# One pipeline over all 96 tiles of a six-layer network, with the attention product written transposed and the bursts of small matmuls joined

## What is computed

```python
qkv = x @ Wqkv;  q, k, v = jnp.split(qkv, 3, -1)      # 16 heads of 64
q = l2norm(q) * qs;  k = l2norm(k) * ksc              # then rotary, with scale
# local_attention: windows of 32 queries, each with its own and the previous 32 keys
sim = jnp.einsum('bhwie,bhwje->bhwij', bq, bk2) * 8.0
sim = jnp.where(mask, -jnp.finfo(sim.dtype).max, sim)
attn = jax.nn.softmax(sim, -1)
out = jnp.einsum('bhwij,bhwje->bhwie', attn, bv2)
x = x + out @ Wo
# feed-forward
xn = (x - mu) / jnp.sqrt(var + 1e-05) * g + bln
a, gate = jnp.split(xn @ W1 + b1, 2, -1)              # 341 + 341 columns
x = x + a * jax.nn.gelu(gate, approximate=False) @ W2 + b2
```

## Time and profile before

| what | value |
|---|---|
| median of 3 executions | 2259.16 us (2250.7 to 2259.73) |
| the profiled execution | 2256.97 us, with a span of 2255.2 us |
| TensorE busy | 1958.2 us, 87% of the span |
| VectorE busy | 1561.8 us, 69% |
| ScalarE busy | 1151.2 us, 51% |
| GpSimd busy | 863.9 us, 38% |
| granted TensorE clock, mean | 0.972 |

### The profile page before, as it was taken

The page is one execution under the profiler, slowest core; times in us unless marked ns, Lnnn a source line. Parts: engine busy times, 40 slices in busy tenths (PEclk is TensorE's granted clock), DMA queues, the critical chain, the costliest instruction groups (busy, mean ns, idle before and its releaser), DMA issues. The chain is left out here.

```text
span 2255.2 us, 71087 instructions
## 1 busy us (share of the span) xinstructions
PE 1958.2 (87%) x31016; PEld 1121.9 (50%) x31016; DVE 1561.8 (69%) x2095; ACT 1151.2 (51%) x1934; POOL 863.9 (38%) x427
## 2 busy tenths in 40 slices
PE   6858889889989898989889898899988888986898
PEld 5635455455545544554555454455544545543444
DVE  6648777777767877777777777778777777863443
ACT  4425555554655555455555555555555555553234
POOL 0225444444434534444443444444445444430000
PEclk9979999999999999999999999999999999997788
DMA  1023222223222322222232222232223222221000
GB/s 42 1 72 93 48 54 60 73 58 75 54 46 56 87 66 58 55 51 67 62 79 50 57 57 74 49 75 62 50 56 86 66 49 56 60 52 43 0 9 10
DMA packets 83885, 124.96 MB, mean 55 GB/s; under 512 B 26112, under 2 KB 31880, under 8 KB 82704
## 3 DMA queue, kind: packets, MB, share of 16 engines
q1 hardware_dynamic: 83600, 120.64, 22.2%
HBM read 21.98 MB, written 1.05 MB: 10 GB/s over the span
## 5 line engine op out<-in xcount | busy, mean ns | idle before, releaser
L352 POOL TENSOR_TENSOR t<-t 128x1024 f32<-128x1024 f32 x192 | 453.3, 2361 | 661.4 <-DVE t L713 661.4
L359 POOL TENSOR_TENSOR qkn<-t,rn 128x1024 f32<-128x1024 f32 x192 | 374.2, 1969 | 373.9 <-DVE rn L737 373.9
L393 PE MATMUL qk_ps<-wqkv,state 128*128 128x512 f32 x768 | 396.5, 599 | 11.5 <-DMA wqkv<-in_w_qkv 9.2
L708 DVE TENSOR_TENSOR t<-qk_ps,rot 128x1024 f32<-128x1024 f32 x192 | 234.5, 1222 | 195.4 <-ACT sq L575 135.5
L404 PEld LDWEIGHTS ring<-ident,qkn 128*128 128x128 f32 x1536 | 180.9, 141 | 198.9 <-issue 122.0
L404 PE MATMUL ring<-ident,qkn 128*128 128x128 f32 x1536 | 233.8, 278 | 26.2 <-POOL qkn L359 25.6
L713 DVE TENSOR_TENSOR t<-qk_ps,rot 128x1024 f32<-128x1024 f32 x192 | 233.1, 1214 | 0.0
L721 DVE TENSOR_REDUCE lnsum<-sq 128x16 f32<-128x1024 f32 x192 | 231.8, 1208 | 0.0
L564 ACT COPY prT<-ring 128x512 f32<-128x512 f32 x192 | 113.2, 590 | 217.2 <-PE ring L438 217.2
L575 ACT ACTIVATE sq<-qk_ps 128x1024 f32<-128x1024 f32 x192 | 198.0, 1031 | 39.0 <-PE qk_ps L393 38.0
L564 ACT COPY oT<-ring 128x512 f32<-128x512 f32 x192 | 112.6, 586 | 184.0 <-PE ring L467 184.0
(11 more groups left out here) (235 smaller groups left out, 2727.2 us busy)
## 6 DMA issues: line engine op xcount, KB each, us to landing
v_win<-v_tok SPq DMA_DIRECT2D x1488, 64.0 KB, 2.0
wqkv<-in_w_qkv SPq DMA_DIRECT2D x6, 1024.0 KB, 5.6
wqkv<-in_w_qkv SPq DMA_DIRECT2D x6, 512.0 KB, 3.7
wo<-in_w_o SPq DMA_DIRECT2D x6, 512.0 KB, 3.8
w<-in_w SPq DMA_DIRECT2D x6, 341.0 KB, 4.0
w<-in_w SPq DMA_DIRECT2D x6, 192.0 KB, 3.9
r_xtok<-in_x SPq DMA_DIRECT2D x4, 256.0 KB, 4.0
amask<-in_att_mask SPq DMA_DIRECT2D x1, 1024.0 KB
```

What stands on the lines that cost most here:

```text
L352: nc.gpsimd.tensor_tensor(t1[:, to], t1[:, to], t2[:, to], ALU.add).then_inc(qk_added.sem, 1)
L359: nc.gpsimd.tensor_tensor(qkn[:, to].rearrange("p (h d) -> p h d", d=DH), t1[:, to].rearrange("p (h d) -> p h d", d=DH), rn[:, HEADS * hal ...
L393: nc.tensor.matmul(qk_ps[:, c, :], tile_of(r, s), wqkv[:, 512 * c:512 * (c + 1)], start=True, stop=True).then_inc(qk_full.sem, 1)
L708: nc.vector.tensor_tensor(t1[:, to].rearrange("p (h d) -> p h d", d=DH), own, rot[:, 2 * half, s:s + 1, :].to_broadcast([P, HEADS, DH]), A ...
```

## The change

The network is rewritten as one loop over stages `g` = 0 to 101 for all engines. In stage `g` tile `g` is projected, tile `g-1` transposed and scored, tile `g-2` put through the softmax, and tile `g-3` multiplied with the values. So the product comes one stage later than before.

- **The product is transposed.** `v_win` is now the stationary operand (64 rows, 64 columns) and `prT` the moving one (32 columns). The result has features on the partitions, as the output projection needs it, and goes to the ring; `transpose_o` and its 8 transposes a tile are gone. Keys 0 to 31 and 32 to 63 with their two halves of the heads are now split by `part`, one ring bank for each. The number of small matmuls stays 64 a tile.
- **The softmax is normalised ahead of the product.** `normalise` on VectorE (two operations of 128x512) is gone; GpSimd multiplies the exponentials by `rden` (`scale_p`, two of 128x512) before they are transposed.
- **The inverse norms** move from VectorE to GpSimd (five operations of 128x32), with one more small operation on ScalarE. GpSimd's product with `rn` is cut from two operations of 128x1024 to four of 128x512.
- **The bursts are joined.** Both halves of `scores` and both halves of `attend` stand one behind the other with nothing between, and because `scores` ends a stage and `attend` opens the next, all 128 small products of the two form one run.
- **The output projection** is made in two halves of 256 columns (steps 1 and 2 of the next round), the normalisation's matmuls in step 3, the feed-forward part in steps 0 and 1 of the round after.
- GpSimd and SyncE are unrolled as well; `rot` is doubled, and weights are loaded with finer waits.

```diff
+        def stage_fills(g):
+            now, turn, prob, att = (tile_there(g - n) for n in range(4))
...
+            fills += [("a", g - 3, f) for f in range(2)] * att
...
+            fills += [("p", g - 2, f) for f in range(2)] * prob
...
+                def inverse_norms(g):
+                    pool.wait_ge(sums_ready, 2 * (g + 1))
+                    nc.gpsimd.tensor_scalar(ss[:, :], sums[:, :], NORM_FLOOR, None, ALU.max).then_inc(newton, 1)
+                    pool.wait_ge(rs_ready, g + 1)
+                    nc.gpsimd.tensor_tensor(nw1[:, :], rs[:, :], rs[:, :], ALU.mult).then_inc(newton, 1)
...
+                def scale_p(g, f):
+                    if f == 0:
+                        pool.wait_ge(rden_ready, g + 1)
...
+                    nc.gpsimd.tensor_tensor(by_head(quarter(pn, f)), by_head(quarter(pe_, f)),
+                                            rden[:, 8 * f:8 * (f + 1)].unsqueeze(2).to_broadcast([P, 8, DH]), ALU.mult).then_inc(p_scaled, 1)
...
-                    for pair in range(4 * f, 4 * (f + 1)):
+                    for pair in range(2 * f, 2 * (f + 1)):
                         for q in range(TW):
                             for par in range(2):
-                                ins = nc.tensor.matmul(
-                                    sc_ps[WIN * q:WIN * (q + 1), par, DH * pair:DH * (pair + 1)],
-                                    prT[64 * par:64 * (par + 1), pair, WIN * q:WIN * (q + 1)],
-                                    v_win[64 * par:64 * (par + 1), TW * t + q, DH * pair:DH * (pair + 1)],
-                                    start=True, stop=True)
+                                n = 2 * pair + par
+                                for part in range(2):
+                                    ins = nc.tensor.matmul(
+                                        to[part][64 * par:64 * (par + 1), P * pair + WIN * q:P * pair + WIN * (q + 1)],
+                                        v_win[64 * part:64 * (part + 1), TW * t + q, DH * n:DH * (n + 1)],
+                                        prT[64 * part:64 * (part + 1), n, WIN * q:WIN * (q + 1)],
+                                        start=True, stop=True)
...
-                def transpose_o(r, s, f):
...
+                for g in range(STAGES):
...
+                    if att:
                         for f in range(2):
+                            attend(g - 3, f)
+                    if now:
                         for f in range(2):
+                            project_q(g, f)
+                    if centre is not None:
+                        ffn_centre(centre)
+                    if turn:
+                        transpose_qk(g - 1, 0)
+                    if down is not None:
+                        ffn_down(down)
...
+                    if prob:
                         for f in range(2):
+                            transpose_p(g - 2, f)
+                    if turn:
+                        for f in range(2):
+                            scores(g - 1, f)
...
+                    for f in range(2):
+                        if prob:
+                            exponentials(g - 2, f)
+                        if att:
+                            copy_o(g - 3, f)
...
+                    if prob:
+                        row_max(g - 2)
+                        row_sum(g - 2)
+                    if now:
+                        rotate(g, 0)
+                    if up is not None:
+                        ffn_gated(up, 0)
+                    if down is not None:
+                        add_ffn(down)
+                    if now:
+                        rotate(g, 1)
...
```

More of the change, by code:

```diff
@@ new lines, in build_network, with bank_of, bank_free @@
+        all_fills = [f for g in range(STAGES) for f in stage_fills(g)]
+        place = {f: n for n, f in enumerate(all_fills)}
+        taken_by = dict(a=(oT_copied, 2), t=(qkT_copied, 4), v=(v_copied, 2), p=(pT_copied, 2), gate=(gelu_ready, 3), lin=(u_ready, 3))
+        def bank_of(*fill):
+            return ring[:, place[fill] % 2, :]
+        def bank_free(*fill):
+            n = place[fill] - 2
+            if n < 0:
+                return None
+            what, of, f = all_fills[n]
+            if what == "wo":
+                return x_attn, 4 * of + 2 * (f + 1)
+            if what == "w2":
+                return x_ffn, 2 * (of + 1)
+            if what == "xc":
+                return xc_copied, of + 1
+            if what == "var":
+                return lnv_ready, of + 1
+            signal, many = taken_by[what]
+            return signal, many * of + f + 1
@@ new lines, in _ @@
+                load_out(0)
+                load_ffn(0)
+                for g in range(TILE_COUNT):
+                    r, t = g // TILES, g % TILES
+                    l, b = r // B, r % B
+                    if t == TILES - 1 and b == B - 1 and l + 1 < DEPTH:
+                        sp.wait_ge(q_full, 2 * (g + 1))
+                        load_qkv(l + 1, 0, s_wq)
+                        sp.wait_ge(k_full, 2 * (g + 1))
+                        load_qkv(l + 1, 1, s_wk)
+                    sp.wait_ge(v_copied, 2 * (g + 1))
@@ L396, in transpose_qk, with project_q @@
-                def transpose_qk(r, s, f):
-                    it, t = r.tile(s, 1)
-                    if f % 2 == 0:
-                        pe.wait_ge(qk_scaled.sem, qk_scaled.at(it, 2 * t + f // 2 + 1))
-                    to = ring_bank(r, "t", s, 1, f)
+                    return bank_of(*fill)
+                def project_q(g, f):
+                    if f == 0:
+                        if g % (B * TILES) == 0:
+                            pe.wait_ge(s_wq, 16 * (g // (B * TILES) + 1))
+                        if g % TILES == 0 and g >= B * TILES:
+                            pe.wait_ge(x_ffn, 2 * (g // TILES - B + 1))
+                        if g > 0:
+                            pe.wait_ge(q_sq, g)
+                            pe.wait_ge(q_rot, 2 * g)
+                    nc.tensor.matmul(qk_ps[:, f, :], tile_of(g), quarter(wqkv, f), start=True, stop=True).then_inc(q_full, 1)
@@ new lines, in project_k, with project_v @@
+                def project_k(g, f):
+                    if f == 0:
+                        if g % (B * TILES) == 0:
+                            pe.wait_ge(s_wk, 16 * (g // (B * TILES) + 1))
+                        if g > 0:
+                            pe.wait_ge(k_sq, g)
+                            pe.wait_ge(k_rot, 2 * g)
+                    nc.tensor.matmul(qk_ps[:, 2 + f, :], tile_of(g), quarter(wqkv, 2 + f), start=True, stop=True).then_inc(k_full, 1)
+                def project_v(g, f):
+                    if f == 0 and g % (B * TILES) == 0:
+                        pe.wait_ge(s_wv, 16 * (g // (B * TILES) + 1))
+                    nc.tensor.matmul(ring_bank("v", g, f), tile_of(g), quarter(wqkv, 4 + f), start=True, stop=True).then_inc(v_full, 1)
```

905 lines of the change are left out of this document (400 added, 505 removed).

## The result

The changed kernel is slower: 2421.54 us, the median of four executions (2414.65 to 2429.81), against 2258.48 for the kernel before. The ratio is 1.072, with a 95% interval of 1.068 to 1.076. I had forecast 2170 us, faster, so the sign was wrong and the miss is 251 us.

A forecast was written before the change was run, and what follows sets the result against it. TensorE's own queue with short waits was taken as the bound. Its terms brought a round from 79.2 to 75.15 us, -97 us in 24 rounds, +8 once, giving 2170 us; 8-in-10 range 2035 to 2258.

The forecast's parts named there:

- Instruction supply: TensorE's joined small matmuls: stops for instruction blocks not yet arrived, 1.5 us a stage, +6.0 us a round.
- one whole block always lies inside the run: Joined scores and product, 2 x 256 instructions: a whole block is used up inside in 1.4 to 1.9 us, every stage.
- 3.9 to 4.4 us from the start of one block to the arrival of the next: Block arrival time, taken from the scores stretch of 2.80 us plus its stops of 1.13 us average, 1.6 at most.
- Clock in full: TensorE's clock in the network: granted in full despite pauses of 1.6 us; no term in the sum.
- Other waits: TensorE's waits for qkn and exponentials shrink, new feed-forward ring waits add some 0.9 us: together -0.7 us a round.
- The product: Product in its new form on TensorE: 1.9 us a tile against 1.73, +0.7 us a round; ends -1.3 and +7.5.
- The rivals on its loads: Product limited by 64-column loads: at their pace, 3.6 us, 2256 us (chance 0.15); without overlap, 2660 us (0.08).
- Scores stretch and normalise: TensorE: scores stretch falls from 2.80 to 1.41 us a tile, -5.6 us a round; wait for normalise goes, -3.35.
- The ends: Pipeline ends: product a stage later, feed-forward part two short stages later, +8 us once.
- GpSimd as the bound: Rival: GpSimd's small operations cost 1.4 us each instead of 0.3 and fill a stage; 2275 us at 1.6, chance 0.04.

The follow-up runs named there:

- mask_between_p: Changed kernel with the two mask matmuls moved between the two groups of transposes of pn; run of 512 kept: 2390.46 us.
- one_q_between: Changed kernel with one q projection between the scores and the product and the other behind the product: 2289.24 us, ratio 1.015.
- scores_split_mask: Changed kernel with q projections separating scores halves and product, first k projection behind the product, first gelu earlier, mask between pn transposes: 2228.66 us, ratio 0.987.

## Why the prediction was wrong

A round came out at 86.45 us for 75.15, 11.3 more. Three steps of the prediction failed: TensorE's clock, put at nothing, cost some 4 us a round; the number of exposed block boundaries was too small, 2.7; and two groups of transposes side by side at the ring, put at nothing, cost 2.2. By the steps of the prediction, in the 19 rounds:

- **Instruction supply, +6.0.** It measured 165.2 / 19 = 8.7, **2.7 more**: 131 stops of 1.56 us over the run, where I had 60 to 96 of 1.5. So the size of a stop was right and their number was not. The step that failed is "one whole block always lies inside the run", taken as one exposed boundary a stage at three quarters of its price. Two boundaries can be exposed in a run of 512, and 131 in 96 stages were, 1.36 a stage. Under it lay "3.9 to 4.4 us from the start of one block to the arrival of the next". That is no fixed time: from the first instruction of a block to the end of the stop behind it the changed kernel has 3.9 us in the median, but 2.4 at the least and 10.6 at 791.00, and the kernel before has 3.0 to 7.8. I had read the right rows: in the earlier trace rows the stop stands behind 54 matmuls, but I timed it from the start of the scores stretch and not from the start of its block, which lay 6.5 us before the stop ended. The Trainium skill ("Runtime: NRT & Kernel Launch", Instruction fetch mechanics) has the fetch of the next block run while the current one executes, and the crossing mostly hidden. The traces agree with the first, and with the second only where slow matmuls fill the 2 to 3 us before a boundary; here 204 us were not hidden.
- **Clock in full.** The last sentence of the prediction named this as a way to be wrong, and the sum had no term for it. The granted clock was 0.95 over the stretch. What the half level cost can be read from the ledger without waits, from 400 to 2000 us (18.5 rounds): 121 of 296 matmuls of the q projections did not run in full clock and took 859 ns to the next start for 456, 48.7 us in all; those of the product lost 20.5 us, all others 6. That is **4.1 a round**, about 98 us in 24. A bound agrees with it: 0.95 means that a tenth of the time, 8.6 us a round, was at half speed, which can cost up to 4.3. As to where it comes from: from 400 to 2000 us the clock is 0.95 in the two kernels that have the whole run of 512 with the new form (the changed one and `mask_between_p`), and 0.98 to 1.00 in all that lack either. A projection inside the run brings it back, even where 112 us of stops stay (`one_q_between`), and so does the old form, with all stops kept. So it takes the unbroken run and the product's 64x64 form; the number of stops does not decide. Whether it is the stops in the run or its length without a full-size matmul, no run separates, and why the form matters stays open.
- **Other waits, -0.7.** The ring cost 100.2 / 19 = 5.3 a round. The ring waits of the kernel before are the three of the earlier trace rows, 50.4 us, and the two smaller ones shown above, in all 68.5 / 19 = 3.6, so I had 2.9, and it is **2.4 more**. Two places: gelu behind its table load, 28.3 / 19 = 1.5, of which I had seen the place and allowed some 0.9 in all; and the second transposes of pn, (15.9 + 9.7 + 8.6 + 8.3) / 19 = 2.2, which I had not seen. "The bursts joined" also put the two groups of these transposes side by side, and I priced that as nothing. The two runs with this part alone give +53 us in the kernel before and -31 us taken out again.
- **The product, +0.7.** In full clock and without its stops (65 of the 96) it took 2.25 a tile to the next matmul for the 1.9 assumed, **1.4 more** a round. Where no stop breaks it, in `scores_split_mask`, it takes 2.0; so most of the excess comes with the stops. The range for it, 1.41 to 3.6, held. The rivals on its loads are out.
- **Scores stretch and normalise, -5.6 and -3.35.** The wait is at nothing. The scores and the transposes of `o_tok` without waits sum to 10.9 a round in the ledger before, and the scores alone to 6.4 after: 4.5 of the 5.6 came, **1.1 less**. A burst of scores took 1.6 us to the next matmul, where the one I had read took 1.41.
- **The ends, +8.** 174 us of the 163 lost lie in the rounds (7.26 x 24), so the ends gave back some 11; this offset some 19 us of the miss.

The four sizes other than the clock, 2.7 + 2.4 + 1.4 + 1.1, leave 3.7 of the 11.3 for it, near the 4.1 read from the ledger. In all 11.3 a round is 271 in 24, less 19: the 251 but for rounding. **GpSimd as the bound** is refuted: its `qkn` cost 5.3 us over the whole run.

The rest of the change, the pipeline, the transposed result and the early normalisation, does pay: 31 us in `scores_split_mask`, which also has gelu earlier. Most of what lost it was that the bursts stand "one behind the other with nothing between".

## What to carry to other kernels

A run of small matmuls is limited by the supply of instructions, in this kernel 256 a block, each of which arrives some 2.5 us after its packet begins, and the packet does not begin when the block before does. In this kernel it was best to keep runs at 128 to 256 instructions, with 0.9 to 1.7 us of full-size matmuls between them. Count matmuls and weight loads, and time the last 200 instructions ahead of any boundary. And when two things are put side by side, price both what now stands behind them without cover and what they were the cover of: three of the edits here that cured one wait opened another at the two-bank ring.

## What the runs showed that I had not expected

- An unbroken run of 512 small instructions with stops in it and the 64x64 form pulled the clock down: 0.71 over 11.8 us of one stage, and q projections of up to 1221 ns where 593 is normal.
- An entry into a burst is cheap: the median from the last full-size matmul's start to the burst's first is 523 ns behind a 512-column projection, where these matmuls normally start 429 ns apart, and 203 ns behind transposes, which start 109 ns apart. So each entry costs 0.09 us, behind either, and not the 0.3 us of the expectations.
- The form with 64 columns stationary and 32 moving passes in 1.85 us per 128 matmuls and loads, the form with 32 and 64 in 1.27 to 1.58; in the fastest kernel the difference is worth only 4 us of the whole, because longer stops take it back.
